# Reordering the TensorE blocks of an attention step: scores, transposes, then probabilities x values

## The chip, the cores and the metric

The kernel runs on one core of a Trainium2 chip. The metric is the device time of one execution in microseconds (us). Before the change the median of three runs is 902.45 us (902.33 to 903.49).

Five engines work side by side and meet only at semaphores: TensorE (PE in the profile, with its weight loads on a row of their own, PEld), VectorE (DVE), ScalarE (ACT), GpSimd (POOL) and SyncE (SP), which issues most of the DMAs. Each engine executes its own instructions in the order in which they are written.

## The reference

A pre-norm block of one attention layer and one feed-forward layer, all in float32, on an input of 2 x 1024 tokens with 1024 features:

```python
# attention: convolution over time, 16 heads of 64, blocks of 128 tokens
x = conv1d(layernorm(inputs), conv_w, width 3) + conv_b   # 1024 -> 3*256
q, k, v = split(x)                                        # blocks of 128 tokens
qh, kh, vh = q @ wq + bq, k @ wk + bk, v @ wv + bv        # 16 heads of 64
scores = where(causal, (qh / sqrt(64)) @ kh.T, -1e9)
o = softmax(scores) @ vh
x1 = inputs + (o @ wo + bo) @ proj_w + proj_b
# feed-forward: a dense layer and four gated low-rank experts
x = layernorm(x1)
out = x1 + x @ W_base.T + b_base + sum_e alpha_e * (x @ A_e.T @ B_e) * 2
```

The products keep nearly full float32 accuracy by splitting each operand into a high and a low part and adding three products (`three_pass`, lines 62 to 64), except in a few places that use plain float32.

## The kernel before, in words

It has three stages. The convolution comes first (to about 328 us of the profile), then the attention (about 326 to 680 us), then the feed-forward layer in 16 tiles of 128 tokens (to the end).

The attention works through 8 groups `g` of 256 tokens (two blocks of 128) and, within a group, 8 pairs of heads `i`. The 64 pairs (`g`, `i`) are numbered J = 8 g + i. A pair passes through a software pipeline: each engine has a function `attention_step(g, i)` that executes, for step J, one stage each of several pairs, and all engines are written in the same rhythm. The constants SC, NRM, TR, PV, OT, AO = 2, 3, 4, 5, 5, 6 say how many steps behind J each stage is. On TensorE a step consists of

- scores of pair J-2 (line 997): q times k, for two heads and two blocks. A head has 64 features, so these matmuls use the array as two row tiles (64\*128 in the profile), one for each head;
- probabilities x values of pair J-5 (line 1008): the weights are 64 columns of values, so the array is used as two column tiles (128\*64);
- transposes of the probabilities of pair J-4 (line 1016): four plain matmuls with the identity over the whole array (128\*128), into the PSUM bank `ptp`;
- q and k of pair J: 12 matmuls of 256 columns over the whole array (lines 62 to 64 by `three_pass`);
- six matmuls of 512 columns, of either the values of this group (`values`) or the output projection of an earlier one (`projection`);
- the product with wo of pair J-6, six matmuls of 256 columns (lines 1051 to 1053).

In what follows these blocks are called scores, PV, transposes, QK, the 512-column block and the wo block.

ScalarE, in its step J, copies the PV result of pair J-5 out of PSUM (line 511, `oT_hi`), then the transposes of pair J-4 (line 516, `pT`), then takes the exponentials of pair J-2 (line 522), copies q and k of pair J with their biases (lines 528 and 529), and does the copies that only some steps have: `c_hi` (533), the values `vf` (538), `a_hi` (543). VectorE computes the masked row maxima (715), the reciprocals of the sums (708) and the low part `oT_lo` (721). GpSimd multiplies the probabilities by the reciprocals (405).

The waits that tie these together: PV of pair j waits for `pT_ready` (its transposes copied), for `oT_lo_ready` of pair j-1 (its PSUM bank read out), and for `v_ready` when the pair is the first or the fifth of a group. The transposes of pair j wait for `p_ready` (GpSimd's product) and for `pT_ready` of pair j-1. No result of PV is used by the transposes of the same step, or the other way round. After the last pair the kernel's attention drains over steps J = 64 to 70, and the first parts of the feed-forward stage (line 808 splits its weights, on VectorE) are interleaved there.

Of the kernel before, what the change touches and what calls it, by code (L numbers as in the profile page):

```python
# [10 lines left out]
ACT = mybir.ActivationFunctionType  # L11
AX_X = mybir.AxisListType.X

P = 128
# [22 lines left out]
def wait(eng, sem, count):  # L37

    if isinstance(count, int) and count <= 0:
        return  # L40
    eng.wait_ge(sem, count)
# [39 lines left out]
def network(nc, ident, x, conv_w, conv_b, wq, wk, wv, wo, pw, bq, bk, bv, bo, pb, w_base, b_base, lora_a, lora_b, router_w, router_b,  # L81
# [38 lines left out]
    UN = 2 * GB  # L120
# [3 lines left out]
    SC, NRM, TR, PV, OT, AO = 2, 3, 4, 5, 5, 6  # L124
# [30 lines left out]
    with ExitStack() as ctx:  # L155
# [25 lines left out]
        pr, pT, mask, negmax, rsum, rrec, ba_c, a_raw, r_raw, act_sb, lbias, logp, lsum, stats, mv, vareps, rstd, logit, fnegmax, expl, esum, erec, alpha, az = \  # L181
# [38 lines left out]
        ptp = psum[:, 3]  # L220
# [23 lines left out]
        s = {n: sp.sem(n) for n in names}  # L244
# [10 lines left out]
        def is_step(jj):  # L255
            return 0 <= jj < NJ
# [191 lines left out]
        def _(act):  # L448
# [55 lines left out]

            def attention_step(g, i):
                J = NP * g + i
                jj = J - OT
                if is_step(jj):
                    act.wait_ge(s["o_done"], jj + 1)
                    wait(act, s["a_step"], jj - 1)  # L510
                    act.activation(oT_hi[:, jj % 2], op.rearrange("p b t -> p (b t)"), ACT.Copy).then_inc(s["oT_hi_ready"], 1)
                jj = J - TR
                if is_step(jj):
                    act.wait_ge(s["pT_done"], jj + 1)
                    wait(act, s["o_done"], jj - 1)
                    act.activation(pT[:, jj % 2].rearrange("p b t -> p (b t)"), ptp, ACT.Copy).then_inc(s["pT_ready"], 1)
                jj = J - SC
                if is_step(jj):
                    act.wait_ge(s["max_ready"], jj + 1)
                    wait(act, s["rrec_ready"], jj - 1)  # L520
                    for un in range(UN):
                        e = act.activation(pr[:, jj % 4, un], pr[:, jj % 4, un], ACT.Exp, bias=negmax[:, jj % 2, un:un + 1], scale=-1.0,  # L522
                                           accum_out=rsum[:, jj % 2, un:un + 1])
                    e.then_inc(s["exp_ready"], 1)
                if is_step(J):
                    act.wait_ge(s["qk_done"], J + 1)
                    wait(act, s["sc_done"], J - 1)
                    act.activation(qf[:, J % 2], qkp[:, 0], ACT.Identity, bias=bqk_c[:, 0, i:i + 1])
                    act.activation(kf[:, J % 2], qkp[:, 1], ACT.Identity, bias=bqk_c[:, 1, i:i + 1]).then_inc(s["qk_ready"], 1)  # L529
                if g + 1 < NG and i in (3, 4):  # L530
                    m = slice(3 * (i - 3), 3 * (i - 3) + 3)
                    act.wait_ge(s["c_loaded"], 16 * (g + 1))
                    act.activation(c_hi[(g + 1) % 2][:, m], c_raw[:, m], ACT.Copy).then_inc(s["c_hi_ready"], 1)
                n = v_unit(g, i)
                if n is not None:
                    k, cols = vcols(n)
                    act.wait_ge(s["v_done"], VT * g + n + 1)
                    act.activation(vf[:, k, cols], vy[n % 2], ACT.Copy).then_inc(s["v_ready"], 1)
                if i == 5 and 0 <= g - 1 < NG:
                    act.wait_ge(s["a_step"], NP * g)  # L540
                    wait(act, s["yy_done"], YT * (g - 1))
                    for d in range(WC):
                        a = act.activation(a_hi[:, d], ap_[:, d], ACT.Identity, bias=ba_c[:, d:d + 1])
                    a.then_inc(s["a_hi_ready"], 1)
                if (g, i) == (0, 4):
                    act.wait_ge(s["wo_loaded"], 16)
                    for k in range(2):
                        act.activation(wo_hi[:, 4 * k:4 * k + 4], wo_raw[:, 4 * k:4 * k + 4], ACT.Copy).then_inc(s["wo_hi_ready"], 1)
                if (g, i) in ((1, 1), (1, 2)):
                    act.wait_ge(s["pw_loaded"], 16)  # L550
                    act.activation(pw_hi[:, i - 1], pw_raw[:, i - 1], ACT.Copy).then_inc(s["pw_hi_ready"], 1)
# [334 lines left out]
        def _(pe):  # L886
# [100 lines left out]
            def attention_step(g, i):  # L987
                J = NP * g + i
                jj = J - SC
                if is_step(jj):  # L990
                    pe.wait_ge(s["qk_ready"], jj + 1)
                    wait(pe, s["max_ready"], jj)
                    for b in range(GB):
                        t = slice(b * P, (b + 1) * P)
                        for h in range(2):
                            e = slice(h * DH, (h + 1) * DH)
                            mm = pe.matmul(scp[:, h, t], qf[e, jj % 2, t], kf[e, jj % 2, t], start=True, stop=True)  # L997
                    mm.then_inc(s["sc_done"], 1)
                jj = J - PV
                if is_step(jj):  # L1000
                    j = jj % NP
                    pe.wait_ge(s["pT_ready"], jj + 1)
                    wait(pe, s["oT_lo_ready"], jj)
                    if j in (0, NP // 2):
                        pe.wait_ge(s["v_ready"], VT * (jj // NP) + (2 if j == 0 else VT))
                    for b in range(GB):
                        for h in range(2):
                            mm = pe.matmul(op[h * DH:(h + 1) * DH, b], vf[:, b, j * P + h * DH:j * P + (h + 1) * DH],  # L1008
                                           pT[:, jj % 2, b, h * P:(h + 1) * P], start=True, stop=True)
                    mm.then_inc(s["o_done"], 1)  # L1010
                jj = J - TR
                if is_step(jj):
                    pe.wait_ge(s["p_ready"], jj + 1)
                    wait(pe, s["pT_ready"], jj)
                    for un in range(UN):
                        mm = pe.transpose(ptp[:, un * P:(un + 1) * P], pr[:, jj % 4, un], ident[:])  # L1016
                    mm.then_inc(s["pT_done"], 1)
                if is_step(J):
                    if J == 0:
                        pe.wait_ge(s["cy_ready"], STEPS - 1)  # L1020
                        pe.wait_ge(s["qk_w_lo_ready"], 2)
                        pe.wait_ge(s["c0_lo_ready"], 1)
                    elif i == 0:
                        pe.wait_ge(s["c_lo_ready"], 2 * g)
                    wait(pe, s["qk_ready"], J)
                    for k in range(2):
                        for c in range(WC):
                            mm = three_pass(pe, qkp[:, k], wqk_hi[:, k, c, i * P:(i + 1) * P], wqk_lo[:, k, c, i * P:(i + 1) * P],
                                            c_hi[g % 2][:, WC * k + c], c_lo[:, g % 2, WC * k + c], c == 0, c == WC - 1)
                    mm.then_inc(s["qk_done"], 1)  # L1030
                n = v_unit(g, i)
                if n is not None:
                    values(g, n)
                yu = y_unit(g, i)
                if yu:
                    projection(*yu)
                if (g, i) == (0, 5):
                    setup_bias()
                jj = J - AO
                if is_step(jj):  # L1040
                    j = jj % NP
                    if jj == 0:
                        pe.wait_ge(s["ba_ready"], 1)
                        pe.wait_ge(s["wo_lo_ready"], 2)
                    elif j == 0:
                        pe.wait_ge(s["a_lo_ready"], jj // NP)
                    pe.wait_ge(s["oT_lo_ready"], jj + 1)
                    for d in range(WC):
                        o = ap_[:, d]
                        col = slice(d * P, (d + 1) * P)  # L1050
                        pe.matmul(o, wo_hi[:, j, col], oT_hi[:, jj % 2], start=j == 0 and d == 0, stop=False, skip_group_check=True)  # L1051
                        pe.matmul(o, wo_hi[:, j, col], oT_lo[:, jj % 2], start=False, stop=False, skip_group_check=True)  # L1052
                        mm = pe.matmul(o, wo_lo[:, j, col], oT_hi[:, jj % 2], start=False, stop=j == NP - 1, skip_group_check=True)  # L1053
                    mm.then_inc(s["a_step"], 1)
# [121 lines left out]
```

## Time and profile before

| | |
|---|---|
| median of 3 runs | 902.45 us (902.33 to 903.49) |
| the profiled execution's own time | 904.03 us |
| its span, first to last instruction | 902.3 us |
| mean granted TensorE clock | 0.988 of full |
| PE busy | 861.6 us, 95% |
| PE weight loads busy | 729.5 us, 81% |
| VectorE, ScalarE, GpSimd busy | 441.8, 395.2, 326.9 us |

The profile names instructions by line, engine and tiles. Matmul ends are modelled, so what counts on TensorE is the distance from the start of one instruction to the start of the next. The timeline view merges equal instructions that follow each other into one row with a count (x8); a float32 matmul that uses a part of the array leaves two records each.

### The profile page before, as it was taken

The numbers are of one execution on the slowest core, as the hardware profiler recorded it, in microseconds if no ns is written. First come the engines' busy times: TensorE is split into PE (matmuls) and PEld (weight loads), VectorE is DVE, ScalarE is ACT, GpSimd is POOL, SyncE is SP. The second block draws the span as 40 slices with busy tenths as digits, with TensorE's granted clock in tenths as the row PEclk, the third lists the DMA queues.
The fourth block names the chain that finished last, engine by engine and source line by source line (L and its number), as shares of the span: only waits on it lengthen the run. The fifth ranks groups of instructions, "written<-read, shape, count | busy, mean of one in ns | idle before, by whom it ended". The sixth has DMA issues, their size and how long they took to land.

```text
span 902.3 us, 14506 instructions
## 1 busy us (share of the span) xinstructions
PE 861.6 (95%) x5376; PEld 729.5 (81%) x5376; DVE 441.8 (49%) x1238; ACT 395.2 (44%) x1024; POOL 326.9 (36%) x295
## 2 busy tenths in 40 slices
PE   3799999998999989999999999999998999999997
PEld 3345788846788878888888888888877999999997
DVE  6844775968564433433333343433365444444442
ACT  5611332642142247876777767676782111101110
POOL 3453857547666302343333343443312100110010
PEclk9899999999999999999999999999999999999999
DMA  6135333225433242012125232120322221322211
GB/s 238 42 124 180 116 94 94 77 58 181 153 93 94 88 170 106 2 36 95 36 95 222 95 89 95 36 95 1 141 80 85 94 78 64 94 94 62 79 48 48
DMA packets 41291, 85.01 MB, mean 94 GB/s; under 512 B 9091, under 2 KB 27523, under 8 KB 40580
## 3 DMA queue, kind: packets, MB, share of 16 engines
q1 hardware_dynamic: 38916, 75.69, 25.5%
q0 software_dynamic: 2304, 8.39, 2.3%
q8 instruction: 43, 0.70, 0.3%
q14 instruction: 28, 0.23, 0.1%
HBM read 60.60 MB, written 23.07 MB: 93 GB/s over the span
## 4 chain that ended last, share of the span: by engine, by line
PE 86%; DVE 6%; ACT 3%; issue 2%; DMA 1%; POOL 1%; DVEq 0%; ACTq 0%
PE net_psum L62 19%; PE net_psum L63 19%; PE net_psum L64 19%; PE net_psum L913 8%; PE net_psum L997 4%; PE net_psum L1008 4%; PE net_psum L1016 4%; PE net_psum L1052 2%; PE net_psum L1053 2%; PE net_psum L1051 2%; PE net_psum L1065 1%; DVE x_lo L661 1%; PE net_psum L895 1%; DVE w_lo L666 1%; PE net_psum L1121 1%
## 5 line engine op out<-in xcount | busy, mean ns | idle before, releaser
L405 POOL TENSOR_TENSOR pr<-pr,rrec 128x512 f32<-128x512 f32 x64 | 66.7, 1042 | 234.3 <-DVE rrec L708 234.3
L62 PE MATMUL net_psum<-fw_hi,xT_hi 128*128 128x354 f32 (+1 forms) x384 | 126.0, 328 | 0.7 <-DVE xT_lo L771 0.7
L64 PE MATMUL net_psum<-fw_hi,xT_lo 128*128 128x354 f32 (+1 forms) x384 | 124.3, 324 | 0.0
L63 PE MATMUL net_psum<-fw_lo,xT_hi 128*128 128x354 f32 (+1 forms) x384 | 124.1, 323 | 0.0
L62 PE MATMUL net_psum<-x_hi,w_hi 128*128 128x512 f32 x288 | 113.5, 394 | 5.3 <-DVE w_lo L666 5.3
L64 PE MATMUL net_psum<-x_hi,w_lo 128*128 128x512 f32 x288 | 112.2, 389 | 0.0
L63 PE MATMUL net_psum<-x_lo,w_hi 128*128 128x512 f32 x288 | 112.1, 389 | 0.0
L522 ACT ACTIVATE pr<-pr,negmax 128x128 f32<-128x128 f32 x256 | 99.0, 391 | 8.5 <-DVE negmax L715 8.5
L473 ACT ACTIVATE w_hi<-raw 128x1024 fp32r<-128x1024 f32 x36 | 38.1, 1058 | 135.1 <-PE net_psum L64 85.5
L666 DVE TENSOR_TENSOR w_lo<-raw,w_hi 128x1024 fp32r<-128x1024 f32 x36 | 51.7, 1437 | 79.1 <-ACT w_hi L473 78.9
L913 PE MATMUL net_psum<-u,raw 128*128 128x512 f32 x192 | 85.8, 609 | 4.8 <-DVE u L650 4.8
L385 POOL TENSOR_TENSOR raw<-raw 128x256 f32<-128x256 f32 x48 | 53.6, 1116 | 95.0 <-DMA raw<-in_conv_w 94.8
L715 DVE CUSTOM_DVE_ANT_0 pr<-net_psum,mask 128x128 f32<-128x128 f32 x256 | 58.8, 285 | 58.9 <-PE net_psum L997 58.9
L62 PE MATMUL net_psum<-c_hi,wqk_hi 128*128 128x256 f32 x256 | 78.5, 307 | 1.9 <-ACT kf L529 1.9
L913 PEld LDWEIGHTS net_psum<-u,raw 128*128 128x128 f32 x192 | 37.4, 196 | 51.4 <-issue 50.5
L64 PE MATMUL net_psum<-c_hi,wqk_lo 128*128 128x256 f32 x256 | 73.3, 286 | 0.0
L63 PE MATMUL net_psum<-c_lo,wqk_hi 128*128 128x256 f32 x256 | 73.3, 286 | 0.0
L62 PEld LDWEIGHTS net_psum<-fw_hi,xT_hi 128*128 128x128 f32 x384 | 72.1, 188 | 1.3 <-DVE xT_lo L771 0.9
L63 PEld LDWEIGHTS net_psum<-fw_lo,xT_hi 128*128 128x128 f32 x384 | 72.3, 188 | 0.0
L64 PEld LDWEIGHTS net_psum<-fw_hi,xT_lo 128*128 128x128 f32 x384 | 72.3, 188 | 0.0
L62 PEld LDWEIGHTS net_psum<-x_hi,w_hi 128*128 128x128 f32 x288 | 54.1, 188 | 17.9 <-DVE w_lo L666 6.6
L438 POOL DMA_DIRECT2D out<-y x16 | 9.4, 585 | 157.8 <-DVE y L804 157.8
(137 smaller groups left out, 1888.9 us busy)
## 6 DMA issues: line engine op xcount, KB each, us to landing
raw<-in_conv_w SPq DMA_DIRECT2D x48, 384.0 KB, 3.5
xn<-in_x SPq DMA_DIRECT2D x16, 512.0 KB, 4.7
xr<-in_x SPq DMA_DIRECT2D x8, 1024.0 KB, 4.9
x_scratch<-xr SPq DMA_DIRECT2D x8, 1024.0 KB, 4.0
x1t<-x_scratch SPq DMA_DIRECT2D x16, 512.0 KB, 4.0
out<-y POOLq DMA_DIRECT2D x16, 512.0 KB, 5.0
c_scratch<-cy SPq DMA_DIRECT2D x12, 512.0 KB, 3.4
c_raw<-c_scratch SPq DMA_DIRECT2D x8, 768.0 KB, 5.1
```

The source lines that it names most:

```text
L62: pe.matmul(out, w_hi, x_hi, start=first, stop=False)
L63: pe.matmul(out, w_hi, x_lo, start=False, stop=False)
L64: return pe.matmul(out, w_lo, x_hi, start=False, stop=last)
L385: pool.tensor_tensor(r[:, :, 3], r[:, :, 1], r[:, :, 2], ALU.add).then_inc(s["sum_ready"], 1)
L405: pool.tensor_tensor(pr[:, jj % 4], pr[:, jj % 4], rrec[:, jj % 4].unsqueeze(2).to_broadcast([P, UN, P]), ALU.mult).then_inc(s["p_ready"], 1)
L473: act.activation(w_hi[:, r % WR], raw[:, k % RR, :, 1:5], ACT.Copy).then_inc(s["w_hi_ready"], 1)
L522: e = act.activation(pr[:, jj % 4, un], pr[:, jj % 4, un], ACT.Exp, bias=negmax[:, jj % 2, un:un + 1], scale=-1.0, accum_out=rsum[:, jj % ...
L666: dve.tensor_tensor(w_lo[:, r % WR], raw[:, k % RR, :, 1:5], w_hi[:, r % WR], ALU.subtract).then_inc(s["w_lo_ready"], 1)
L715: m = dve.tensor_tensor_reduce(out=pr[:, jj % 4, un], in0=scp[:, h, b * P:(b + 1) * P], in1=mask[:], scale=-DH ** -0.5, scalar=-MASKED, op ...
L913: mm = pe.matmul(acc[st % 2][:, v, :], raw[:, k % RR, c % 2, 1 + v], u[:, c, v], start=c == 0, stop=c == DC - 1)
L997: mm = pe.matmul(scp[:, h, t], qf[e, jj % 2, t], kf[e, jj % 2, t], start=True, stop=True)
L1008: mm = pe.matmul(op[h * DH:(h + 1) * DH, b], vf[:, b, j * P + h * DH:j * P + (h + 1) * DH], pT[:, jj % 2, b, h * P:(h + 1) * P], start=Tru ...
```

## The change

On TensorE the transposes of pair J-4 are moved ahead of the PV block of pair J-5, right behind the scores. On ScalarE the copy of the transposes (`pT`) is moved ahead of the copy of the PV result (`oT_hi`). All waits and signals go with their instructions; none is added or removed.

```diff
@@ ScalarE, attention_step @@
                 J = NP * g + i
+                jj = J - TR
+                if is_step(jj):
+                    act.wait_ge(s["pT_done"], jj + 1)
+                    wait(act, s["o_done"], jj - 1)
+                    act.activation(pT[:, jj % 2].rearrange("p b t -> p (b t)"), ptp, ACT.Copy).then_inc(s["pT_ready"], 1)
                 jj = J - OT
                 if is_step(jj):
                     act.wait_ge(s["o_done"], jj + 1)
                     wait(act, s["a_step"], jj - 1)
                     act.activation(oT_hi[:, jj % 2], op.rearrange("p b t -> p (b t)"), ACT.Copy).then_inc(s["oT_hi_ready"], 1)
-                jj = J - TR
-                if is_step(jj):
-                    act.wait_ge(s["pT_done"], jj + 1)
-                    wait(act, s["o_done"], jj - 1)
-                    act.activation(pT[:, jj % 2].rearrange("p b t -> p (b t)"), ptp, ACT.Copy).then_inc(s["pT_ready"], 1)
@@ TensorE, attention_step @@
                     mm.then_inc(s["sc_done"], 1)
+                jj = J - TR
+                if is_step(jj):
+                    pe.wait_ge(s["p_ready"], jj + 1)
+                    wait(pe, s["pT_ready"], jj)
+                    for un in range(UN):
+                        mm = pe.transpose(ptp[:, un * P:(un + 1) * P], pr[:, jj % 4, un], ident[:])
+                    mm.then_inc(s["pT_done"], 1)
                 jj = J - PV
                 if is_step(jj):
...
                     mm.then_inc(s["o_done"], 1)
-                jj = J - TR
-                if is_step(jj):
-                    pe.wait_ge(s["p_ready"], jj + 1)
-                    wait(pe, s["pT_ready"], jj)
-                    for un in range(UN):
-                        mm = pe.transpose(ptp[:, un * P:(un + 1) * P], pr[:, jj % 4, un], ident[:])
-                    mm.then_inc(s["pT_done"], 1)
```

On TensorE, in a step in the middle of the attention, lines with - stand only in the kernel before and lines with + only in the changed one. L997 are the scores, L1008 (L1015 in the changed kernel) the PV block, L1016 (L1004) the transposes, and the last rows the beginning of QK:

```order
 L997 MATMUL net_psum<-kf,qf 128x128 [waits net_max_ready,net_qk_ready]
 L997 MATMUL net_psum<-kf,qf 128x128 x3
-L1008 MATMUL net_psum<-pT,vf 64x128 [waits net_oT_lo_ready,net_pT_ready]
-L1008 MATMUL net_psum<-pT,vf 64x128 x3
-L1016 MATMUL net_psum<-ident,pr 128x128 [waits net_pT_ready,net_p_ready]
-L1016 MATMUL net_psum<-ident,pr 128x128 x3
+L1004 MATMUL net_psum<-ident,pr 128x128 [waits net_pT_ready,net_p_ready]
+L1004 MATMUL net_psum<-ident,pr 128x128 x3
+L1015 MATMUL net_psum<-pT,vf 64x128 [waits net_oT_lo_ready,net_pT_ready]
+L1015 MATMUL net_psum<-pT,vf 64x128 x3
 L62 MATMUL net_psum<-c_hi,wqk_hi 128x256 [waits net_qk_ready]
 L63 MATMUL net_psum<-c_lo,wqk_hi 128x256
```

The blocks in column tiles (64x128) stood between the row-tiled scores and the transposes; they now stand between two blocks that use the whole array.

On ScalarE, in a step in the middle of the attention, the kernel before has (oT_hi is the copy of the PV result, pT that of the transposes, pr the exponentials, qf and kf the copies of q and k):

```order
L511 ACTIVATE oT_hi<-net_psum 128x256 [waits net_a_step,net_o_done]
L516 ACTIVATE pT<-net_psum 128x512 [waits net_o_done,net_pT_done]
L522 ACTIVATE pr,rsum<-pr,negmax 128x128 [waits net_rrec_ready,net_max_ready]
L522 ACTIVATE pr,rsum<-pr,negmax 128x128 x3
L528 ACTIVATE qf<-net_psum,net_bqk_c 128x256 [waits net_sc_done,net_qk_done]
L529 ACTIVATE kf<-net_psum,net_bqk_c 128x256
```

and the changed one:

```order
L511 ACTIVATE pT<-net_psum 128x512 [waits net_o_done,net_pT_done]
L516 ACTIVATE oT_hi<-net_psum 128x256 [waits net_a_step,net_o_done]
L522 ACTIVATE pr,rsum<-pr,negmax 128x128 [waits net_rrec_ready,net_max_ready]
L522 ACTIVATE pr,rsum<-pr,negmax 128x128 x3
L528 ACTIVATE qf<-net_psum,net_bqk_c 128x256 [waits net_sc_done,net_qk_done]
L529 ACTIVATE kf<-net_psum,net_bqk_c 128x256
```

Only the first two have changed places. The instructions of the other three engines stand as before.

## Rows read from the trace of the kernel before

**Rows 1.** The page, part 1: busy us (share of the span) xinstructions

```profile
PE 861.6 (95%) x5376; PEld 729.5 (81%) x5376; DVE 441.8 (49%) x1238; ACT 395.2 (44%) x1024; POOL 326.9 (36%) x295
```

**Rows 2.** Stages: us, busy of PE, PEld, DVE, ACT, POOL, PEclk, DMA

```profile
345.00:400.00 55.00, 54.92 (x460) 48.91 (x458) 21.46 (x109) 42.22 (x144) 20.41 (x15) 0.97 0.17 59
...
600.00:657.00 57.00, 57.00 (x466) 49.92 (x466) 19.65 (x114) 40.75 (x142) 20.10 (x15) 1.00 0.15 57
```

**Rows 3.** Waits of PEld, 360 to 657 us: us in total, times, longest

```profile
PEld net_psum L1016 <- issue: 9.6, 56, 0.2
PEld net_psum L1008 <- issue: 1.4, 6, 0.2
```

**Rows 4.** Timeline of PE, one step: start us, us, line, tiles, xcount [idle before]

```profile
561.12 0.71 PE L997 MATMUL net_psum<-kf,qf 64*128 64x128 f32 x8
561.77 0.66 PE L1008 MATMUL net_psum<-pT,vf 128*64 128x128 f32 x8
562.36 0.66 PE L1016 MATMUL net_psum<-ident,pr 128*128 128x128 f32 x4
562.77 0.36 PE L62 MATMUL net_psum<-c_hi,wqk_hi 128*128 128x256 f32 x1
562.97 0.28 PE L63 MATMUL net_psum<-c_lo,wqk_hi 128*128 128x256 f32 x1
```

**Rows 5.** Timeline of PEld, weight loads of the same step

```profile
562.36 0.42 PEld L1016 LDWEIGHTS net_psum<-ident,pr 128*128 128x128 f32 x4 [0.17 <-issue]
562.74 0.19 PEld L62 LDWEIGHTS net_psum<-c_hi,wqk_hi 128*128 128x128 f32 x1
```

**Rows 6.** Timeline of PE, same step: last PV and last transpose alone

```profile
562.15 0.27 PE L1008 MATMUL net_psum<-pT,vf 128*64 128x128 f32 x1
...
562.74 0.27 PE L1016 MATMUL net_psum<-ident,pr 128*128 128x128 f32 x1
```

**Rows 7.** Timeline of PE, step 4, where no PV stands between

```profile
335.78 0.40 PE L64 MATMUL net_psum<-wv_hi,c_lo 128*128 128x512 f32 x1
336.11 0.71 PE L997 MATMUL net_psum<-kf,qf 64*128 64x128 f32 x8
336.75 0.33 PE L1016 MATMUL net_psum<-ident,pr 128*128 128x128 f32 x1
```

**Rows 8.** Timeline of PE, step 68: the last PV block, no transposes behind it

```profile
672.94 0.66 PE L1008 MATMUL net_psum<-pT,vf 128*64 128x128 f32 x8 [0.86 <-DVE oT_lo L721]
673.53 0.39 PE L1051 MATMUL net_psum<-oT_hi,wo_hi 128*128 128x256 f32 x1
673.75 0.28 PE L1052 MATMUL net_psum<-oT_lo,wo_hi 128*128 128x256 f32 x1
```

**Rows 9.** Timeline of PE, step 5, the first PV block

```profile
342.99 0.66 PE L1008 MATMUL net_psum<-pT,vf 128*64 128x128 f32 x8 [1.54 <-ACT vf L538]
...
344.19 0.28 PE L63 MATMUL net_psum<-c_lo,wqk_hi 128*128 128x256 f32 x1
```

**Rows 10.** Timeline of PE, step 53: first PV block of a group

```profile
598.55 0.72 PE L997 MATMUL net_psum<-kf,qf 64*128 64x128 f32 x8
599.35 0.66 PE L1008 MATMUL net_psum<-pT,vf 128*64 128x128 f32 x8
```

**Rows 11.** Timeline of ACT: step 52's values copy; step 47's copies and exponential

```profile
598.61 0.59 ACT L538 ACTIVATE vf<-net_psum 128x512 f32<-128x512 f32 x1
...
567.82 0.39 ACT L511 ACTIVATE oT_hi<-net_psum 128x256 fp32r<-128x256 f32 x1 [1.05 <-PE net_psum L1008]
568.40 0.60 ACT L516 ACTIVATE pT<-net_psum 128x512 f32<-128x512 f32 x1 [0.19 <-PE net_psum L1016]
568.89 0.39 ACT L522 ACTIVATE pr<-pr,negmax 128x128 f32<-128x128 f32 x1
```

**Rows 12.** Timeline of POOL: product of the pair transposed at 567.71

```profile
563.14 1.04 POOL L405 TENSOR_TENSOR pr<-pr,rrec 128x512 f32<-128x512 f32 x1 [5.15 <-DVE rrec L708]
```

**Rows 13.** The stretch at the attention's end, columns as in Rows 2

```profile
667.30:678.90 11.60, 9.53 (x70) 8.10 (x69) 11.50 (x16) 9.02 (x16) 1.49 (x2) 1.00 0.49 181
```

## The prediction, made before the changed kernel ran

> **What bounds the kernel now.** I read the page's busy line first: TensorE is busy for 861.6 of 902.3 us, all others for less than half [rows 1]. The stages say where the changed code runs and what limits it there: between 600 and 657 us PE is busy for all 57.00 us at the full clock (2.4 GHz), ScalarE for 40.75, VectorE for 19.65 [rows 2]. So in the attention nothing but TensorE's own sequence counts, and a wait on another engine is worth only what it leaves on that sequence. The third view, the waits of the weight loads, is the telling one: before the transposes there is a gap in 56 steps, 9.6 us together, for which no other engine is named ("issue"), and 6 gaps before PV blocks, 1.4 us [rows 3]. The fourth view is the timeline of one step, read by starts.
>
> In it the scores start at 561.12, PV at 561.77, the transposes at 562.36, the first QK matmul at 562.77 and the second at 562.97 [rows 4]: 0.65 + 0.59 + 0.41 + 0.20 = 1.85 us. Two kinds of borders are in that sum. Where the array's tiling changes, the next weight load doesn't start under the matmuls in flight: the last PV matmul (column tiles) starts at 562.15 and the load of the transposes (whole array) only at 562.36, 0.21 later, after 0.17 of idling [rows 5, 6]. Where it doesn't change, there is no such gap: the last transpose starts at 562.74, and in the same hundredth QK's weight load [rows 5, 6], so that the first QK matmul follows at 562.77.
>
> The Trainium skill says the same in "TensorEngine Tiling (Array Packing)", Key Properties: a change of the tiling mode, not just of the tile, drains TensorE. Rows 5 and 6 agree, with 0.21 us at the change and none without.
>
> **The change part by part.** Before, a step has three changes of tiling: wo block to scores, scores to PV, PV to transposes; the transposes then run into QK without one. After, it has four: wo block to scores, scores to transposes, transposes to PV, PV to QK. No instruction is added. The new sequence is summed from borders that the trace has elsewhere:
>
> - scores to transposes: step 4 has no PV yet, and there it is 336.11 to 336.75, 0.64 [rows 7];
> - transposes to PV: not in the trace. The last transpose starts 0.38 after the first (562.36 to 562.74), and a drained load follows 0.21 after the last matmul [rows 4 to 6]: 0.59. From below: if this border cost no more than transposes to QK, PV would follow after 0.41 [rows 4]. From above: the longest drain in the rows is 335.78 to 336.11, 0.33 behind a matmul of 512 columns [rows 7], which gives 0.71. A gain is excluded, since 0.41 is already the border without a drain. I take 0.59, because the last matmul here has 128 columns, as in the row with 0.21;
> - PV to a block on the whole array: step 68 has PV without transposes behind it, 672.94 to 673.53, 0.59, and the second matmul 0.22 later [rows 8].
>
> The sum is 0.64 + 0.59 + 0.59 + 0.22 = 2.04 us against 1.85. The hundredths leave 0.19 or 0.20; I take 0.195. It is paid on the critical engine in steps 6 to 63, 58 steps: **+11.3 us** (bounds: 58 x 0.01 = 0.6 and 58 x 0.315 = 18.3).
>
> Three small gains stand against it.
>
> - First PV of a group. The PV block also waits there for the values, which ScalarE copies in the step before: the copy runs 598.61 to 599.20 [rows 11], and PV starts 0.80 after the scores instead of 0.65 [rows 10]. With the transposes ahead, PV starts 0.64 + 0.59 = 1.23 after the scores, 599.78, and the values are there. This saves 0.15 in each of groups 1 to 7 (six show as gaps [rows 3]): **-1.05 us**. Bounds: 0 to -1.05.
> - Step 5. PV waits for the first values until 342.99, after 1.54 of idling, and the transposes and QK come behind it; the second QK matmul is at 344.19 [rows 9], 1.20 later. The transposes now fill the wait, and what follows 342.99 is 0.59 + 0.22 = 0.81: **-0.4 us**.
> - The attention's end. From 667.3 to 678.9 VectorE is busy for 11.50 of 11.60 us while PE has 9.53 [rows 13]. It splits the feed-forward weights there, and PE's drains in steps 64 to 67 lie beside that and cost nothing. What starts this part is the exponential behind the two copies on ScalarE. Each copy starts 0.3 us behind the last matmul of its block (one step of 5.35 us after 562.15 and 562.74 it is 567.50 and 568.09, and the copies start at 567.82 and 568.40 [rows 6, 11]), and the second block ends at the same distance from the scores in either order (0.64 + 0.59 against 0.65 + 0.59). The copy that now comes last takes 0.39 instead of 0.60 [rows 11], so the exponentials start 0.2 earlier: **-0.2 us** here. Earlier, in each step, the same 0.2 only widens the cover.
>
> What stays hidden. ScalarE's pair of copies: 0.2 us a step less in front of the exponentials, and QK 0.2 later in front of the q and k copies; ScalarE has 16 idle us in 57 [rows 2]. `oT_lo` comes 0.7 later, but the wo block that needs it is in the next step. The wait for GpSimd's product is met 0.59 earlier than before: the product of pair 43 ends at 564.18 [rows 12], and its transposes start some 0.7 before their copy at 568.40 [rows 11], at about 567.7. A cover of 3.5 us shrinks to 2.9; without it each missing tenth would cost a tenth. No queue of DMAs is moved past.
>
> Sum: 11.3 - 1.05 - 0.4 - 0.2 = +9.65 us. The profiled execution took 904.03 us, 1.7 outside its span and 1.58 above the median of the runs; nothing of that is changed, so it would come to 913.7, and the median of 902.45 to **912.1 us**.
>
> **The rivals.**
>
> *No drain at the new border.* The transposes' weights are the probabilities and PV's are values; if the loads of PV could be pulled under the last transposes, the step would be 0.64 + 0.41 + 0.59 + 0.22 = 1.86, 0.6 us over 58 steps, and with the three gains the time would be 902.45 + 0.6 - 1.65 = 901.4: no change. For it: QK's load does exactly that behind the transposes [rows 5]. Against it: QK has the transposes' tiling and PV has not, and each border in the rows at which the tiling changes has the gap.
>
> "TensorE: Matmul & The Clock Gate" of the Trainium skill, Step-by-step: what each phase is for, lets the engine pull a weight load ahead of matmuls in flight if it targets the background weight buffer or other row groups. Taken alone, this rule stands for the rival; the trace agrees with it only at borders without a change of tiling.
>
> *Faster.* The drain is tied to the pair of blocks and not to the tiling, so that neither transposes to PV nor PV to QK has one. Then PV to QK would be 0.41 + 0.20 too: 0.64 + 0.41 + 0.41 + 0.20 = 1.66, 0.19 less than before, -11.0 - 1.65, 889.8 us. It decides if PV to QK falls under 0.59. Against it stands the 0.59 between PV and a block on the whole array [rows 8].
>
> *The clock.* A step now holds four gaps of 0.2 us in about 5.5. If the granted clock falls to 1.2 GHz in some stretches of the attention, each costs what a mean of 0.97 over 55 us costs now (3.3 us at half speed, 1.65 lost) [rows 2]. Three such stretches give 917. Against it: three gaps a step leave the clock at 1.00 [rows 2].
>
> *A dearer border.* At the upper bound of 0.71 for transposes to PV, the time is 912.1 + 58 x 0.12 = 919.1.
>
> **How the numbers follow.** The forecast gets 0.87, no drain 0.05, faster 0.02, the clock 0.04, the dearer border 0.02. Its own range is 910.0 to 914.5: 0.18 to 0.21 a step move it by 0.9, a part of the first gain may stay away (1.05), and the runs before spread over 1.2 us. To hold the time 8 times in 10 with the sizes of borders at a hundredth I widen that a little, 909.5 to 915.0. A measurement of this kernel tells 0.2%, 1.8 us, from no change. Slower by more: 0.93; within: 0.05; faster: 0.02.
>
> **What would show it.** In the profile after: scores to second QK matmul 2.04 instead of 1.85, with a load of PV that starts 0.2 after the last transpose and a gap in front of QK's first load instead of in front of the transposes; no wait for the values in a group's first PV; scores of step 64 later by some 9.9 us; VectorE as full as now at the end; clock 1.00 in the middle. If transposes to PV shows 0.41, the first rival holds. If the step shows 2.04 and the time is still not 9 us up, a wait on PE that I don't see has been absorbed, and the reading of the stages was wrong.

## The result, and the profile after

| | before | changed |
|---|---|---|
| median of 4 runs | 902.97 us (902.33 to 904.42) | 913.03 us (911.08 to 913.79) |
| ratio to before | | 1.0106, 95% interval 1.0085 to 1.0127 |
| profiled execution, span | 904.03, 902.3 us | 911.08, 909.3 us |
| mean granted clock in it | 0.988 | 0.992 |

The kernel became 1.1% slower, 10 us, where 912.1 (909.5 to 915.0) was forecast. The kernel before has one run more here than in its first table, hence 902.97 instead of 902.45. The profiled execution of the changed kernel is its fastest one; the section on the prediction says why it lies low.

One step of TensorE, in the timeline (start, duration, line, tiles, count); the rows answer to [rows 4]:

```profile
566.63 0.71 PE L997 MATMUL net_psum<-kf,qf 64*128 64x128 f32 x8
567.28 0.66 PE L1004 MATMUL net_psum<-ident,pr 128*128 128x128 f32 x4
567.87 0.66 PE L1015 MATMUL net_psum<-pT,vf 128*64 128x128 f32 x8
568.45 0.39 PE L62 MATMUL net_psum<-c_hi,wqk_hi 128*128 128x256 f32 x1
568.68 0.28 PE L63 MATMUL net_psum<-c_lo,wqk_hi 128*128 128x256 f32 x1
```

From the scores to the second QK matmul it is 0.65 + 0.59 + 0.58 + 0.23 = 2.05 us, against 1.85 in rows 4. The weight loads of the same step show what the 0.20 is; they answer to [rows 5]:

```profile
567.28 0.42 PEld L1004 LDWEIGHTS net_psum<-ident,pr 128*128 128x128 f32 x4
567.86 0.42 PEld L1015 LDWEIGHTS net_psum<-pT,vf 128*64 128x64 f32 x8 [0.17 <-issue]
568.45 0.19 PEld L62 LDWEIGHTS net_psum<-c_hi,wqk_hi 128*128 128x128 f32 x1 [0.17 <-issue]
```

The one marked gap of before, ahead of the transposes, is gone, and two have come, ahead of PV and ahead of QK. The last transpose starts at 567.66 (the next row, cut out by a narrow window, answers to the second of [rows 6]), and PV's load 0.20 later:

```profile
567.66 0.27 PE L1004 MATMUL net_psum<-ident,pr 128*128 128x128 f32 x1
```

The steps in the middle of the attention are all alike. The waits of the weight loads between 380 and 660 us have the gaps of 50 steps twice, and no other [rows 3]. That is one marked gap per step more than before, and two of the four changes of tiling, those ahead of the scores and behind them, are marked in neither kernel:

```profile
PEld net_psum L62 <- issue: 8.7, 51, 0.2
PEld net_psum L1015 <- issue: 8.4, 50, 0.2
```

The first PV block of a group no longer waits for its values. In step 53, scores, transposes and PV start at the usual distances (PV 1.24 after the scores), while the copy of the values, on ScalarE, ends at 605.67, a microsecond before [rows 10, 11]:

```profile
605.41 0.71 PE L997 MATMUL net_psum<-kf,qf 64*128 64x128 f32 x8
606.06 0.66 PE L1004 MATMUL net_psum<-ident,pr 128*128 128x128 f32 x4
606.65 0.55 PE L1015 MATMUL net_psum<-pT,vf 128*64 128x128 f32 x6
```

```profile
605.08 0.59 ACT L538 ACTIVATE vf<-net_psum 128x512 f32<-128x512 f32 x1
```

Step 5 has its transposes inside the wait for the first values, and QK's second matmul follows PV by 0.82 instead of 1.20 [rows 9]:

```profile
342.92 0.66 PE L1015 MATMUL net_psum<-pT,vf 128*64 128x128 f32 x8 [0.96 <-ACT vf L538]
343.51 0.39 PE L62 MATMUL net_psum<-c_hi,wqk_hi 128*128 128x256 f32 x1
343.74 0.28 PE L63 MATMUL net_psum<-c_lo,wqk_hi 128*128 128x256 f32 x1
```

ScalarE, in the step whose scores start at 572.17, has its two copies without a pause between them and the exponentials 2.22 us behind the scores [rows 11]:

```profile
573.51 0.60 ACT L511 ACTIVATE pT<-net_psum 128x512 f32<-128x512 f32 x1 [1.24 <-PE net_psum L1004]
574.11 0.38 ACT L516 ACTIVATE oT_hi<-net_psum 128x256 fp32r<-128x256 f32 x1
574.39 0.40 ACT L522 ACTIVATE pr<-pr,negmax 128x128 f32<-128x128 f32 x1
```

The stages, with the columns of [rows 2]: TensorE is as full as before in the middle and VectorE as full at the end [rows 13]. The clock is 1.00 in the first stretch, where it was 0.97 [rows 2]:

```profile
345.00:400.00 55.00, 54.69 (x454) 46.74 (x454) 21.01 (x109) 42.52 (x144) 20.41 (x15) 1.00 0.17 59
600.00:657.00 57.00, 57.00 (x460) 48.13 (x460) 18.91 (x107) 38.78 (x133) 19.65 (x14) 1.00 0.21 75
676.05:687.65 11.60, 10.31 (x74) 8.67 (x72) 11.44 (x16) 9.24 (x15) 1.49 (x2) 1.00 0.48 181
```

### The profile page after: what moved, and what is told of

Same layout as the page of the kernel before. It is cut to its first block, busy times and chain, and to the rows that moved or that the text cites. A ratio compares the mean times of both kernels' runs of the same rounds, so it can differ in the third digit from the quotient of the medians.

```text
span 909.3 us, 14506 instructions
## 1 busy us (share of the span) xinstructions
PE 870.1 (96%) x5376; PEld 728.0 (80%) x5376; DVE 442.6 (49%) x1238; ACT 396.1 (44%) x1024; POOL 316.5 (35%) x295
## 4 chain that ended last, share of the span: by engine, by line
PE 86%; DVE 6%; ACT 3%; issue 2%; DMA 1%; POOL 1%; DVEq 0%; ACTq 0%
PE net_psum L62 20%; PE net_psum L63 19%; PE net_psum L64 19%; PE net_psum L913 8%; PE net_psum L997 4%; PE net_psum L1015 4%; PE net_psum L1004 4%; PE net_psum L1051 2%; PE net_psum L1052 2%; PE net_psum L1053 2%; PE net_psum L1065 1%; DVE x_lo L661 1%; PE net_psum L895 1%; DVE w_lo L666 1%; ACT pr L522 1%
## 5 line engine op out<-in xcount | busy, mean ns | idle before, releaser
L385 POOL TENSOR_TENSOR raw<-raw 128x256 f32<-128x256 f32 x48 | 55.5, 1156 | 103.4 <-DMA raw<-in_conv_w 103.3
L511 ACT ACTIVATE pT<-net_psum 128x512 f32<-128x512 f32 x64 | 38.3, 598 | 92.3 <-PE net_psum L1004 92.2
```

Of the source, the lines that this page charges most:

```text
L385: pool.tensor_tensor(r[:, :, 3], r[:, :, 1], r[:, :, 2], ALU.add).then_inc(s["sum_ready"], 1)
```

## The experiments

The theory: each change of the array's tiling makes the next weight load wait until about 0.2 us after the last matmul's start, and the new order has four such changes in a step instead of three. Its rivals: ScalarE's new order carries part of the loss; the loss belongs to the one border from transposes to PV; or it belongs to PV itself. Steps below are the distance between the scores of successive steps in the middle of the attention, from the timeline: 5.35 us before, 5.54 in the changed kernel. Each experiment is told from the kernel that its heading sentence names, each ratio is to the kernel before on the same chip, and in the diffs whole blocks stand for their code.

### One half of the change at a time

TensorE's half alone, from the kernel before:

```diff
  TensorE: scores
+ TensorE: transposes
  TensorE: PV
- TensorE: transposes
  ScalarE: oT_hi, pT     (as before)
```

> Only TensorE's half of the change: scores, transposes, PV on TensorE, while ScalarE still copies the PV result before the transposes. Theory (a fourth change of the array's tiling per step costs 0.19 to 0.20 us of TensorE): steps of 5.54 us as in the changed kernel, 2.04 from the scores to the second QK matmul, 911.5 to 914 us. Rival (ScalarE's new order carries a good part of the loss): clearly less than the changed kernel's loss of 10 us, 903 to 909.

Measured: 914.63 us (914.05 to 915.80), ratio 1.0122 (1.0097 to 1.0147), steps of 5.54 us, and in its timeline the scores, transposes and PV at the distances of the changed kernel:

```profile
567.27 0.71 PE L997 MATMUL net_psum<-kf,qf 64*128 64x128 f32 x8
567.91 0.66 PE L1004 MATMUL net_psum<-ident,pr 128*128 128x128 f32 x4
568.50 0.66 PE L1015 MATMUL net_psum<-pT,vf 128*64 128x128 f32 x8
572.81 0.38 PE L997 MATMUL net_psum<-kf,qf 64*128 64x128 f32 x2
```

The whole loss is TensorE's. The median is 0.6 above the expected range. ScalarE, which waits for PV first here, starts its exponentials later in a step (575.50 for the scores at 572.81, 2.69 instead of 2.22), and the attention's end hangs on them: the first dense matmul follows the scores of step 64 by 18.22 us (666.99 to 685.21) instead of 17.46. The intervals of the two ratios overlap, so these 0.8 us are read from the timeline, not from the times.

ScalarE's half alone, from the kernel before:

```diff
  TensorE: scores, PV, transposes     (as before)
+ ScalarE: pT
  ScalarE: oT_hi
- ScalarE: pT
```

> Only ScalarE's half: the copy of the transposes ahead of the copy of the PV result, TensorE as in the kernel before. Theory: ScalarE now waits longer before its first copy and its exponentials start 0.3 us later, but TensorE does not wait for it: steps of 5.35 us, 902 to 904.5 us. Rival (ScalarE's order carries the loss): 906 to 913.

Measured: 905.62 us (904.19 to 906.63), ratio 1.0021 (1.0009 to 1.0032). The expectation missed: a microsecond above its range, though far from the rival. Its ordinary steps are 5.35 us. But the first PV of a group waits for the values, and now names them; in step 53 it starts 1.06 us after the scores instead of 0.80 [rows 10]:

```profile
600.58 0.71 PE L997 MATMUL net_psum<-kf,qf 64*128 64x128 f32 x8
601.64 0.66 PE L1008 MATMUL net_psum<-pT,vf 128*64 128x128 f32 x8 [0.35 <-ACT vf L538]
```

```profile
600.91 0.59 ACT L538 ACTIVATE vf<-net_psum 128x512 f32<-128x512 f32 x1
```

ScalarE is 0.27 us later in each step, since it waits for the transposes before it copies a PV result that has long been there. I had said that TensorE doesn't wait for ScalarE; it does, in six steps of the 58. Those six take 5.77 instead of 5.50, 1.6 us of the 2; another 0.3 is at the attention's end, where the first dense matmul follows the scores of step 64 by 17.92 instead of 17.66.

The next kernel tests this reading. It starts from ScalarE's half alone, with the copy of the values put ahead of the copy `c_hi`:

```diff
  ScalarE, attention_step, steps 3 and 4 of a group:
+ vf <- values      (0.59 us)
  c_hi <- c_raw     (0.84 us)
- vf <- values
```

> Only ScalarE's half of the change (the kernel of e2) with the copy of the values ahead of c_hi (the edit of e6). It tells what made six steps of e2 5.77 us long. Theory (ScalarE's new order under TensorE's old one makes ScalarE 0.3 us later in every step; TensorE notices only where the first PV of a group waits for the values): with the values 0.84 us earlier the long steps are gone, all steps 5.35, 901 to 903 us, 3 to 4 less than e2. Rival (the late transposes' copy itself holds TensorE): the six steps stay above 5.5, 904 or more.

Measured: 902.74 us (899.68 to 905.12), ratio 0.9999 (0.9981 to 1.0018). All steps are 5.35 and the long ones are gone: for the steps the reading holds. The time agrees with it but doesn't carry it alone. By the ratios the edit brought 0.2%, 2.0 us (1.0021 against 0.9999, on two chips and each within 0.1 to 0.2%), less than the 3 to 4 expected. By the trace this kernel should be some 1.3 us faster than the kernel before, since it has lost that one's six waits (0.9) and 0.7 of step 5 and pays 0.3 at the attention's end; the ratio shows no gain, with an interval that reaches down to 0.9981.

### Fewer and more changes of tiling

From the changed kernel, with ScalarE in the changed order: transposes ahead of the scores. They are then in one run with the wo block of the step before, and the step has three changes again, though PV still comes behind the transposes:

```diff
+ TensorE: transposes
  TensorE: scores
- TensorE: transposes
  TensorE: PV
```

> Transposes ahead of the scores, so TensorE's order is wo block, transposes, scores, PV, QK; ScalarE in the changed order. PV still comes behind the transposes, but the step has three changes of tiling again. Theory: from the last wo matmul to the second QK matmul 2.10 us against 2.06 before and 2.25 in the changed kernel (the drain in front of QK exposes a load of 0.19 us, that in front of the transposes one of 0.14); +0.045 x 58 = +2.6, the waits of the first PV blocks and of step 5 gone (-1.45): about 904, 902.5 to 905.5. Rival (what costs is PV coming behind the transposes, not the count of tiling changes): like the changed kernel, 911 to 914.

Measured: 904.52 us (902.76 to 905.96), ratio 1.0007 (0.9994 to 1.0020), steps of 5.40.

```profile
562.43 0.29 PE L1053 MATMUL net_psum<-oT_hi,wo_lo 128*128 128x256 f32 x1
562.55 0.60 PE L994 MATMUL net_psum<-ident,pr 128*128 128x128 f32 x4
563.08 0.71 PE L1004 MATMUL net_psum<-kf,qf 64*128 64x128 f32 x8
563.72 0.66 PE L1015 MATMUL net_psum<-pT,vf 128*64 128x128 f32 x8
564.31 0.38 PE L62 MATMUL net_psum<-c_hi,wqk_hi 128*128 128x256 f32 x1
564.53 0.28 PE L63 MATMUL net_psum<-c_lo,wqk_hi 128*128 128x256 f32 x1
```

The first transpose follows the last wo matmul after 0.12, the ordinary distance, and the sum to the second QK matmul is 0.12 + 0.53 + 0.64 + 0.59 + 0.22 = 2.10. The same number of changes is not quite the same time, 5.40 against 5.35. The expectation had this from the loads: behind the drain ahead of QK a load of 0.19 us comes bare [rows 5], behind the one ahead of the transposes a load of 0.14, as the kernel before has it when one load is cut out by a narrow window:

```profile
562.36 0.14 PEld L1016 LDWEIGHTS net_psum<-ident,pr 128*128 128x128 f32 x1 [0.17 <-issue]
```

The size fits, but no run varies the length of the load alone, so this reason is not shown. The rival at 911 to 914 is out. This kernel also has two marked gaps a step, as many as the changed one, ahead of the scores and ahead of QK, and yet the time of three changes: the marks don't count the changes.

From the kernel before: PV ahead of the scores, three changes as well, ending with the transposes like the kernel before:

```diff
+ TensorE: PV
  TensorE: scores
- TensorE: PV
  TensorE: transposes
```

> PV ahead of the scores: wo block, PV, scores, transposes, QK, three changes of tiling as before; ScalarE in the order of before. Theory: 2.06 us from the last wo matmul to the second QK matmul, as before, and steps of 5.35; but PV of a group's first pair comes 0.65 earlier and so waits 0.80 instead of 0.15 for the values: seven steps of 6.15, and step 5 0.65 longer: +4.5 + 0.65 = +5.2, 906.5 to 909.5. Rival (any order other than the one before costs about 0.2 per step): 912 or more.

Measured: 908.28 us (907.08 to 909.28), ratio 1.0050 (1.0035 to 1.0064). Ordinary steps are 5.35, six of the seven steps with a group's first PV are 6.14, and that block names what it waits for. The seventh, in the last group, takes 5.49: there is no `c_hi` to copy ahead of its values. The expectation had counted seven long ones:

```profile
602.19 0.28 PE L1053 MATMUL net_psum<-oT_hi,wo_lo 128*128 128x256 f32 x1
603.19 0.66 PE L998 MATMUL net_psum<-pT,vf 128*64 128x128 f32 x8 [0.72 <-ACT vf L538]
603.78 0.71 PE L1009 MATMUL net_psum<-kf,qf 64*128 64x128 f32 x8
```

So three orders with three changes take 5.35 to 5.40 a step, and what they differ in otherwise is the wait for the values.

From the changed kernel, with ScalarE in the changed order: PV in two halves around the transposes, five changes with the same matmuls:

```diff
  TensorE: scores
- TensorE: transposes
- TensorE: PV
+ TensorE: PV of block 0
+ TensorE: transposes
+ TensorE: PV of block 1
```

> PV in two halves with the transposes between them (scores, PV of block 0, transposes, PV of block 1, QK): five changes of tiling per step, the same matmuls. ScalarE in the changed order. Theory: one more drain than the changed kernel, 0.15 us since each half of PV is a short block of its own: 2.19 from the scores to the second QK matmul, steps of 5.69, 902.5 + 58 x 0.345 = 922.5, range 920.5 to 924.5. Rival (the loss belongs to the one border transposes to PV, however many others there are): as the changed kernel, 911 to 914.

Measured: 926.99 us (922.71 to 927.43), ratio 1.0256 (1.0232 to 1.0280). The steps of its profiled execution are 5.69, as expected, and there are three marked gaps in each (columns as in [rows 3]):

```profile
PEld net_psum L62 <- issue: 8.4, 49, 0.2
PEld net_psum L1015 <- issue: 8.4, 49, 0.2
PEld net_psum L1022 <- issue: 8.2, 49, 0.2
```

That execution took 922.71, the 922.5 of the expectation, but the median missed the expected range, 2.5 us above its upper end. The other four took 924.8 to 927.4. Three of them had a lower mean granted clock (0.984 to 0.986 against 0.988 in the profiled one), but the one of 924.84 had 0.990, so the clock alone doesn't explain them, and only one execution was profiled. The fifth change shows in the steps, 0.15 us each; 4 to 5 us of this kernel's median stay open.

### PV without column tiles

From the changed kernel. Both heads' products go to the same rows here, so the output is not the reference's:

```diff
- pe.matmul(op[h * DH:(h + 1) * DH, b], vf[:, b, j * P + h * DH:j * P + (h + 1) * DH],
+ pe.matmul(op[:, b], vf[:, b, j * P:(j + 1) * P],
```

> The changed order, with PV's weights taken as 128 columns (the values of both heads) instead of 64, so that PV uses the whole array and needs no column tiles. Both heads write the same 128 rows of PSUM, and only the second head's product is kept; the output is not the reference's. PV runs twice as many matmul passes one after another (no two column tiles side by side), about 0.87 us instead of 0.39. Theory (the gap belongs to the change of tiling): no gap before PV's or QK's weight loads; one gap per step is left there, in front of the transposes behind the row-tiled scores; scores to second QK matmul 2.0 to 2.1 us. Rival (the gap belongs to PV, its operands or its place between transposes and QK): gaps of about 0.2 us before PV and QK stay, and scores to second QK is 2.4 to 2.5.

Measured: 921.65 us in a single execution. The weight loads of one step:

```profile
564.09 0.42 PEld L1004 LDWEIGHTS net_psum<-ident,pr 128*128 128x128 f32 x4
564.47 0.97 PEld L1015 LDWEIGHTS net_psum<-pT,vf 128*128 128x128 f32 x8
565.37 0.19 PEld L62 LDWEIGHTS net_psum<-c_hi,wqk_hi 128*128 128x128 f32 x1
```

Same blocks in the same order, PV reading 128 columns of the same values instead of 64, and not one marked gap in the attention: PV's load starts 0.38 after the first load of the transposes, which is where the last transpose starts. QK's load, which the edit doesn't touch, has lost its gap too. So the gaps belong to the change of tiling and not to PV's place. The gap that the expectation left in front of the transposes isn't marked, here or in the changed kernel; the transposes follow the scores after 0.65 in both. The step isn't shorter for it, since PV now takes 0.9 us instead of 0.39; scores to second QK matmul is 2.15 (5.65 a step), a little over the 2.0 to 2.1 expected.

### A version faster than both

From the kernel before, with the values' copy ahead of `c_hi` (the edit shown above):

> The kernel before, with one edit on ScalarE: the copy of the values (vf) goes ahead of the copy c_hi in steps 3 and 4 of a group, so the values of a group are there 0.84 us earlier. Theory (the first PV of each group waits 0.15 us for them, and the first one of all 1.54): the seven steps of 5.50 us become 5.35, step 5 gets 0.8 shorter: -1.05 - 0.8 = -1.9 us, 900.3 to 902. Rival (the 0.15 is something else at these steps): the steps of 5.50 stay, and at most step 5 gets shorter, 902 to 903.

Measured: 901.03 us (899.51 to 904.97) against 904.23 on the same chip, ratio 0.9977 (0.9962 to 0.9991). All steps are 5.35. The 0.23% are 2.1 us, where 1.9 was expected. In step 53:

```profile
596.16 0.71 PE L997 MATMUL net_psum<-kf,qf 64*128 64x128 f32 x8
596.80 0.66 PE L1008 MATMUL net_psum<-pT,vf 128*64 128x128 f32 x8
```

PV is back at 0.64 behind the scores. In the changed kernel the same edit finds only the wait of step 5 to save:

> The changed kernel with the copy of the values ahead of c_hi. Theory: its steps of 5.54 us have no wait for the values left, so they stay 5.54; only step 5, where the first values come after a wait of 1.0, gets up to 0.8 us shorter: 911.5 to 913.5. Rival (part of the 5.54 is still a wait for ScalarE): steps under 5.5 and under 910 us.

Measured: 912.14 us (909.52 to 912.51), ratio to before 1.0097 (1.0059 to 1.0134), steps of 5.54, so no part of them was a wait for the values. The distance from the scores of step 5 to those of step 6 is 8.59 instead of 9.34, as expected.

## Why the prediction was right

The time came to 913.03 against 912.1, the ratio to 1.0106 against 912.1 / 902.45 = 1.0107. By its own steps:

- Scores to transposes, 0.64 from step 4: measured 0.65.
- Transposes to PV, the one border that the trace before didn't have, taken as 0.59 between bounds of 0.41 and 0.71: measured 0.59 (567.28 to 567.87), with PV's load 0.20 after the last transpose. The rival with 0.41 is refuted by this row, and the whole-array PV shows under which condition it would have held.
- PV to QK, 0.59 + 0.22 from step 68: measured 0.58 + 0.23.
- The step: 0.195 more forecast; steps of 5.54 against 5.35 are 0.19.
- First PV of a group, -1.05: the waits are gone, but there were six and not seven of them, so this term was 0.9. In the kernel before, the steps with a group's first PV take 5.50 in groups 1 to 6 and 5.35 in group 7, where no `c_hi` is copied ahead of the values. The transposes to its front alone did that; ScalarE's order worked the same way (without TensorE's half it worked against it, 0.27 in each).
- Step 5, -0.4: 0.82 instead of 1.20, that is -0.38.
- The attention's end, -0.2: the first dense matmul starts 17.46 us after the scores of step 64 instead of 17.66. The four rows below are the scores of step 64 and that matmul, the first two of before, the others of the changed kernel.

```profile
657.52 0.71 PE L997 MATMUL net_psum<-kf,qf 64*128 64x128 f32 x8
...
675.18 0.43 PE L62 MATMUL net_psum<-fw_hi,xT_hi 128*128 128x354 f32 x1 [0.67 <-DVE xT_lo L771]
```

```profile
666.35 0.72 PE L997 MATMUL net_psum<-kf,qf 64*128 64x128 f32 x8
...
683.81 0.43 PE L62 MATMUL net_psum<-fw_hi,xT_hi 128*128 128x354 f32 x1 [0.68 <-DVE xT_lo L771]
```

One figure of the forecast looks wrong in these rows: the scores of step 64 are later by 8.8 us, not by 9.9. The clock makes the difference, and with it the profiled execution's low time. In the kernel before, a stretch at 1.2 GHz lies at 351.7 to 355.1 us (the 0.97 of [rows 2]; 256-column matmuls start 0.21 apart there instead of 0.12), behind the matmuls of a single column in the bias set-up at 346.90 to 350.45, and it is missing in the changed kernel's profiled execution, which has the same matmuls; step 6 got shorter by 0.8 instead of longer by 0.2, which is the 1.0. A second one is missing in the feed-forward stage. The two rows are the same 16 us of work, 26.5 us behind the scores of step 64, before and after:

```profile
684.00:700.00 16.00, 12.72 (x61) 10.63 (x60) 8.21 (x20) 2.78 (x6) 0.56 (x1) 0.89 0.28 91
```

```profile
692.80:708.80 16.00, 12.71 (x71) 11.05 (x70) 9.68 (x24) 2.60 (x6) 0.55 (x1) 1.00 0.28 91
```

A mean of 0.89 over 16 us is 3.5 us at half speed, some 1.7 lost. Neither stretch has to do with the change: TensorE's half alone and the changed kernel with the values first, with TensorE in the changed order, have 0.97 between 345 and 400 us and 0.97 between 670 and 720, like the kernel before. So the profiled pair differs by 7.0 us in span where the medians differ by 10; the other three runs of the changed kernel, at clocks of 0.988 to 0.990, took 912.8 to 913.8. The medians of 902.97 and 913.03 bear out the sum; the 913.7 that it gave for the profiled execution missed by 2.6, for the clock.

What the prediction had wrong was its reason for leaving ScalarE out. "Nothing but TensorE's own sequence counts" held for the pair of edits together. ScalarE's edit alone costs 0.2% (1.0009 to 1.0032), as the second experiment showed, because the copy of the values is already 0.15 us late in six steps, and there whatever else ScalarE loses is added to TensorE's time. The forecast had the number of that wait, and used it only for TensorE's half. That didn't matter to the time of the pair, in which the copy ends a microsecond before PV.

## What to carry to other kernels

On TensorE, count the changes of tiling in a loop before moving a block: a block of row or column tiles that stands between blocks on the whole array pays at both of its ends, one beside a block that is tiled another way shares a border. Here each additional change cost 0.15 to 0.20 us, in an engine that is busy all the time, and none of the busy shares shows it. The weight loads' gaps for which no engine is named point at it, but they don't count it: the kernel before has one in a step with three changes, the transposes-first kernel two with as many changes and nearly the same time. Count the changes in the code, and take their price from the distances of the starts. A border that a trace doesn't have can be put together from borders that it has, if the prologue and the drained end of a pipeline are read too, since blocks are missing there.

## What the runs showed of the hardware

- The price of a change of tiling isn't the same everywhere: with three changes each, a step took 5.35 us where the last one is ahead of the transposes (two orders), and 5.40 where it is ahead of QK. The bare load (0.14 and 0.19 us) is the likely reason, not a shown one.
- Float32 matmuls with 64 columns of weights in two column tiles took 0.39 us where the same products on the whole array took 0.9; here this outweighs the drains that the tiles bring, 5.54 against 5.65 us a step.
- More gaps on TensorE did not lower the clock in the middle of the attention: between 600 and 657 us it was 1.00 with three, four and five changes of tiling a step in the profiled executions.
